# A second layer norm and router placed inside a rotary attention's tile pipeline

## The reference, cut to what matters

```
z = cond2(x)                       # dense and typed experts, mixed by a gate
z = z + attn(layernorm(z, ln1))    # convolution, rotary attention, 16 heads of 16, causal
z = z + moe(layernorm(z, ln2))     # 4 experts, each token goes to one of them
out = x + z

def _layernorm(x, w, b):
    mu = jnp.mean(x, axis=-1, keepdims=True)
    var = jnp.mean((x - mu) ** 2, axis=-1, keepdims=True)
    return (x - mu) * jax.lax.rsqrt(var + EPS) * w + b

def _moe(x, ln_w, ln_b, router_w, expert_wv, expert_proj):
    h = _layernorm(x, ln_w, ln_b)
    expert_idx = jnp.argmax(h @ router_w, axis=-1)
    ...
```

## Time and profile before

| what | value |
|---|---|
| median of 3 runs | 2254.34 us (2252.97 to 2255.35) |
| the profiled execution | 2255.13 us |
| its span, first to last instruction | 2253.3 us |
| mean granted TensorE clock | 0.956 |
| TensorE busy in the span | 2053.0 us, 91% |
| VectorE / ScalarE / GpSimd busy | 50% / 42% / 30% |
| rotary attention's tile loop | some 1876 to 1975 us |
| second norm and router | 1976 to 2017 us |
| sort and routed experts | 2017 us to the end |

### The profile page before, as it was taken

The page is one execution under the profiler, slowest core; times in us unless marked ns, Lnnn a source line. Parts: engine busy times, 40 slices in busy tenths (PEclk is TensorE's granted clock), DMA queues, the critical chain, the costliest instruction groups (busy, mean ns, idle before and its releaser), DMA issues. The chain is left out here.

```text
span 2253.3 us, 32388 instructions
## 1 busy us (share of the span) xinstructions
PE 2053.0 (91%) x11764; PEld 1725.6 (77%) x11764; DVE 1120.4 (50%) x1969; ACT 941.9 (42%) x1879; POOL 666.2 (30%) x713
## 2 busy tenths in 40 slices
PE   7999999999999999999998666899899666868998
PEld 6888888888888888888886455688799455747998
DVE  3333443434344344434435785423477566756775
ACT  4242323323232332424224697322355354555664
POOL 3030200203030120303100396110388143308884
PEclk9999999999999999999999698899899878978999
DMA  4010010101001010200001200410156123246661
GB/s 160 1 57 1 1 56 0 56 0 56 0 11 45 0 56 0 81 0 0 1 1 38 53 36 31 149 38 10 53 198 195 41 44 109 78 142 206 212 215 57
DMA packets 93436, 139.98 MB, mean 62 GB/s; under 512 B 15438, under 2 KB 70384, under 8 KB 93360
## 3 DMA queue, kind: packets, MB, share of 16 engines
q1 hardware_dynamic: 86304, 122.97, 17.1%
q0 software_dynamic: 4928, 12.86, 1.6%
q10 hardware_dynamic: 2128, 3.15, 0.4%
HBM read 106.96 MB, written 12.06 MB: 53 GB/s over the span
## 5 line engine op out<-in xcount | busy, mean ns | idle before, releaser
L584 DVE TENSOR_TENSOR cond_h<-cond_silu,ps 128x512 f32<-128x512 f32 x288 | 197.9, 687 | 697.6 <-ACT cond_silu L495 694.1
L495 ACT ACTIVATE cond_silu<-ps 128x512 f32<-128x512 f32 x288 | 172.3, 598 | 772.6 <-PE ps L414 772.6
L414 PE MATMUL ps<-a_x_hi,cond_w_hi 128*128 128x512 f32 x1152 | 449.8, 390 | 2.0 <-DVE a_x_lo L262 2.0
L414 PE MATMUL ps<-a_x_lo,cond_w_hi 128*128 128x512 f32 x1152 | 449.3, 390 | 0.0
L414 PE MATMUL ps<-a_x_hi,cond_w_lo 128*128 128x512 f32 x1152 | 449.1, 390 | 0.0
L383 POOL TENSOR_TENSOR cond_w_lo<-cond_stage_up,cond_w_hi 128x256 fp32r<-128x256 f32 x144 | 108.6, 771 | 833.7 <-ACT cond_w_hi L476 833.7
L414 PEld LDWEIGHTS ps<-a_x_hi,cond_w_hi 128*128 128x128 f32 x1152 | 216.9, 188 | 47.5 <-DVE a_x_lo L262 2.4
L414 PEld LDWEIGHTS ps<-a_x_hi,cond_w_lo 128*128 128x128 f32 x1152 | 216.9, 188 | 45.3
L414 PEld LDWEIGHTS ps<-a_x_lo,cond_w_hi 128*128 128x128 f32 x1152 | 216.9, 188 | 45.0
L430 PE MATMUL ps<-cond_h_hi,cond_d_hi 128*128 128x512 f32 x576 | 224.4, 390 | 3.4 <-DVE cond_h_lo L552 3.4
L430 PE MATMUL ps<-cond_h_hi,cond_d_lo 128*128 128x512 f32 x576 | 224.1, 389 | 0.0
(11 more groups left out here) (371 smaller groups left out, 4086.4 us busy)
## 6 DMA issues: line engine op xcount, KB each, us to landing
moe_stage_up<-in_L_ffn_expert_wv SPq DMA_DIRECT2D x22, 1024.0 KB, 8.4
typed_stage_up<-in_L_cond_wi SPq DMA_DIRECT2D x11, 1024.0 KB, 4.9
typed_stage_dn<-in_L_cond_wo SPq DMA_DIRECT2D x11, 1024.0 KB
moe_stage_dn<-in_L_ffn_expert_proj SPq DMA_DIRECT2D x11, 1024.0 KB
cond_stage_up<-in_L_cond_Wg SPq DMA_DIRECT2D x7, 1024.0 KB, 4.8
cond_stage_up<-in_L_cond_Wu SPq DMA_DIRECT2D x7, 1024.0 KB, 6.8
cond_stage_dn<-in_L_cond_Wd SPq DMA_DIRECT2D x7, 1024.0 KB, 5.1
hyp_v_now<-hyp_v_blk SPq DMA_DIRECT2D x16, 272.0 KB, 2.3
```

The source lines that it names most:

```text
L414: ins = pe.matmul(up_ps[st % 2][j], w[:, j, k, fs], x[:, k, tok], start=(i == 0), stop=(i == 3 * KC - 1))
L495: act.activation(silu[:, st % 2], up_ps[st % 2][0], ACT.Silu).then_inc(act_done, 1)
L584: dve.tensor_tensor(h[:, st % 2], silu[:, st % 2], up_ps[st % 2][1], ALU.mult).then_inc(up_free, 1)
```

## The change

The stage `layer_norm` is gone. Its work is done tile by tile in the rotary attention's pipeline, in token rows. `out` now takes the turned y as the stationary operand, so that its result has tokens on the partitions, and adds the residual by two matmuls with the identity. VectorE reads that result for bn_stats and bn_aggr (`stats`, `aggr`), ScalarE makes the inverse root by Ln and Exp (`rstd`), VectorE norms (`norm`) and adds x (`total`), GpSimd multiplies by w and adds b (`weigh`), TensorE turns h (`h_turn`), ScalarE copies it (`h_take`), TensorE makes the logits (`route`), VectorE keeps them (`keep`). SP copies the residual and x for each tile (`bring_sum`) and stores a tile's rows (`store`). The pipeline has 22 steps instead of 20, 8 of them ahead of the loop instead of 6. The choice is made once for all tokens behind the last tile; the first slot's weights are loaded at the start of `routed_ffn`.

```diff
+class Router:
+    def __init__(self, nc, ctx, ln_w, ln_b, w_r, x_rows, table, sel):
...
+        self.loads = [(self.w[:], wide(ln_w)), (self.b[:], wide(ln_b)), (self.wr[:], w_r.rearrange("(k p) e -> p k e", p=P))]
...
             lag = dict(bring=0, turn=1, q_blk=1, k_blk=1, score=1, clamp=2, top=2, shift=2, prob=2, p_turn=3, p_take=3,
-                       mix=3, y=3, y_turn=4, y_take=4, out=4, add=4, fetch=1)
-            order = dict(tensor="y_turn p_turn out turn mix score", scalar="y_take p_take q_blk prob",
-                         vector="clamp top add k_blk y", gpsimd="shift", sync="bring fetch")
+                       mix=3, y=3, y_turn=4, y_take=5, out=5, fetch=1, bring_sum=4, stats=5, aggr=5, rstd=5, norm=5, total=5,
+                       weigh=5, h_turn=6, h_take=6, route=6, keep=6, store=6)
+            order = dict(tensor="out p_turn h_turn turn mix score route y_turn",
+                         scalar="y_take p_take h_take q_blk rstd prob",
+                         vector="clamp top stats k_blk aggr norm total y keep", gpsimd="shift weigh",
+                         sync="bring fetch bring_sum store")
...
+            hT_ps, lg_ps = m.bank[0][:, D:2 * D], m.bank[1][:, D:D + E_MOE]
...
+                    def bring_sum(i, q, nth):
+                        wait(sp, out_done, i - 1)
+                        sp.dma_start(router.res[:, q], resT[:, :, bass.ds(i * P, P)]).then_inc(sum_brought[q], 16)
+                        wait(sp, added, i - 1)
+                        sp.dma_start(router.x[:, q], router.x_rows[bass.ds(i * P, P)]).then_inc(sum_brought[q], 16)
+                    def store(i, q, nth):
+                        sp.wait_ge(weighed, i + 1)
+                        sp.wait_ge(added, i + 1)
+                        sp.dma_start(router.table[bass.ds(i * P, P)], router.rows[:, q]).then_inc(stored[q], 16)
+                    if not hyper:
+                        router.load(sp)
+                    run(sp, "sync", dict(bring=bring, fetch=fetch, bring_sum=bring_sum, store=store))
...
                         wait(pe, k_blocked, i)
+                        if not hyper:
+                            wait(pe, kept, i - 5)
                         for c in range(KC):
...
                         wait(pe, q_taken, i)
+                        if not hyper:
+                            wait(pe, h_taken, i - 4)
                         for c in range(KC):
...
                         wait(pe, added, i)
+                        if not hyper:
+                            wait(pe, normed, i)
...
                     def out(i, q, nth):
                         pe.wait_ge(y_taken, i + 1)
                         wait(pe, added, i)
+                        if not hyper:
+                            wait(pe, normed, i)
+                            pe.wait_ge(sum_brought[q], 32 * (nth + 1))
+                            for k in range(KC):
+                                pe.matmul(o_ps, yT[:, q, k], wo[:, k], start=(k == 0), stop=False)
+                            for c in range(KC):
+                                ins = pe.matmul(o_ps[:, c * P:(c + 1) * P], router.res[:, q, c], m.ident, start=False, stop=(c == KC - 1))
+                            ins.then_inc(out_done, 1)
+                            return
                         for c in range(KC):
                             for k in range(KC):
                                 ins = pe.matmul(o_ps[:, c * P:(c + 1) * P], wo[:, k, c * P:(c + 1) * P], yT[:, q, k],
                                                 start=(k == 0), stop=(k == KC - 1))
                         ins.then_inc(out_done, 1)
 
+                    def h_turn(i, q, nth):
+                        pe.wait_ge(weighed, i + 1)
+                        wait(pe, h_taken, i)
+                        wait(pe, q_taken, i + 5 if not isinstance(i, int) else min(i + 5, NP))
+                        for c in range(KC):
+                            ins = pe.transpose(hT_ps[:, c * P:(c + 1) * P], router.rows[:, q, c * P:(c + 1) * P], m.ident)
+                        ins.then_inc(h_turned, 1)
+                    def route(i, q, nth):
+                        pe.wait_ge(h_taken, i + 1)
+                        wait(pe, kept, i)
+                        wait(pe, k_blocked, i + 6 if not isinstance(i, int) else min(i + 6, NP))
+                        for c in range(KC):
+                            ins = pe.matmul(lg_ps, router.hT[:, q, c], router.wr[:, c], start=(c == 0), stop=(c == KC - 1))
+                        ins.then_inc(routed, 1)
+                    if not hyper:
+                        pe.wait_ge(router.loaded, 16 * len(router.loads))
+                    run(pe, "tensor", dict(turn=turn, score=score, p_turn=p_turn, mix=mix, y_turn=y_turn, out=out, h_turn=h_turn, route=route))
...
+                    def inverse(i, q, nth):
+                        act.wait_ge(averaged, i + 1)
+                        wait(act, normed, i - 1)
+                        act.activation(router.rstd[:, q:q + 1], router.mean[:, q, 1:2], ACT.Ln, bias=router.eps[:]).then_inc(logged, 1)
+                        act.wait_ge(logged, i + 1)
+                        act.activation(router.rstd[:, q:q + 1], router.rstd[:, q:q + 1], ACT.Exp, scale=-0.5).then_inc(rstd_done, 1)
+                    def h_take(i, q, nth):
+                        act.wait_ge(h_turned, i + 1)
+                        wait(act, routed, i - 1)
+                        act.activation(router.hT[:, q].rearrange("p c n -> p (c n)"), hT_ps, ACT.Copy).then_inc(h_taken, 1)
+                    if not hyper:
+                        act.preload_act_table_set("natural_log_exp_and_others")
+                        act.wait_ge(eps_set, 1)
...
+                        if not hyper and not isinstance(i, int):
+                            dve.wait_ge(gathered, i + 1 + lag["k_blk"] - lag["stats"])
...
+                    def statistics(i, q, nth):
+                        dve.wait_ge(out_done, i + 1)
+                        wait(dve, rstd_done, i - 1)
+                        dve.bn_stats(router.stats[:, q], o_ps).then_inc(gathered, 1)
+                    def aggregate(i, q, nth):
+                        if isinstance(i, int):
+                            dve.wait_ge(gathered, i + 1)
+                        dve.bn_aggr(router.mean[:, q], router.stats[:, q]).then_inc(averaged, 1)
+                    def normalize(i, q, nth):
+                        dve.wait_ge(rstd_done, i + 1)
+                        wait(dve, weighed, i - 1)
+                        dve.tensor_scalar(router.xn[:, q], o_ps, router.mean[:, q, 0:1], router.rstd[:, q:q + 1],
+                                          ALU.subtract, ALU.mult).then_inc(normed, 1)
+                    def total(i, q, nth):
+                        dve.wait_ge(sum_brought[q], 32 * (nth + 1))
+                        wait(dve, stored[q], 16 * nth)
+                        dve.tensor_tensor(router.rows[:, q, D:], o_ps, router.x[:, q], ALU.add).then_inc(added, 1)
+                    def keep(i, q, nth):
+                        dve.wait_ge(routed, i + 1)
+                        dve.tensor_copy(router.logits[:, bass.ds(i, 1)].rearrange("p o e -> p (o e)"), lg_ps).then_inc(kept, 1)
+                    phases = dict(stretch=stretch, k_blk=block_k, clamp=clamp, top=top, y=scale_y, add=add)
+                    if not hyper:
+                        phases = dict(k_blk=block_k, clamp=clamp, top=top, y=scale_y, stats=statistics, aggr=aggregate, norm=normalize, total=total, keep=keep)
+                    run(dve, "vector", phases)
+                    if not hyper:
+                        dve.wait_ge(kept, NP)
+                        router.choose(dve, chosen)
...
+                    def weigh(i, q, nth):
+                        pool.wait_ge(normed, i + 1)
+                        wait(pool, stored[q], 16 * nth)
+                        wait(pool, h_turned, i - 1)
+                        pool.tensor_tensor(router.xn[:, q], router.xn[:, q], router.w[:], ALU.mult).then_inc(scaled, 1)
+                        pool.wait_ge(scaled, i + 1)
+                        pool.tensor_tensor(router.rows[:, q, 0:D], router.xn[:, q], router.b[:], ALU.add).then_inc(weighed, 1)
...
-def layer_norm(nc, m, tag, srcT, ln_w, ln_b, router, sync_late):
...
     def sync(self, sp):
+        self.slots.load_slot(sp, 0, 0)
...
-            attention(nc, m, "rope", False, s0, m.sumT, rope)
+            second.close()
+            router = Router(nc, s, a["L0_ffn_ln2_w"], a["L0_ffn_ln2_b"], a["L0_ffn_router_w"], typed_table, moe_table, m.moe_sel)
+            attention(nc, m, "rope", False, s0, m.sumT, rope, router, moe_stored)
...
-            with ExitStack() as f:
-                rows = f.enter_context(nc.sbuf_tensor("moe_rows", [P, NP, 2 * D], F32))
-                layer_norm(nc, m, "ln2", m.sumT, a["L0_ffn_ln2_w"], a["L0_ffn_ln2_b"],
```

(56 more changed lines are left out.)

189 lines of the change are left out of this document (18 added, 171 removed).

## The result

The changed kernel takes 2299.33 us (median of four, 2296.64 to 2301.72) against 2254.85 (four, 2252.97 to 2259.67): a ratio of 1.0194, 95% interval 1.0173 to 1.0215, so 44.5 us slower. The forecast was 2273.0 with a range up to 2288: the sign and the mechanism came, the size did not. The profiled execution took 2296.64 us, span 2294.8, 41.5 more than before; the clock's mean fell from 0.956 to 0.947.

The account below looks back on a forecast made before the run. Bound before: the ring of VectorE and the scores, 5.46 us a step. Loop 43.7 + drain 13.4 + loads 1.5 + choice 1.8 + barrier 0.9 - removed stage 42.4 = +18.9 us, giving 2273 us, range 2255 to 2288.

Parts of the forecast that it names:

- the sign: Whole kernel: the change makes it slower, +18.9 us; slower by more than 4.5 us given 0.80.
- the mechanism: Rotary attention loop: out waits about 2 us each time for copies queued on SP behind the fetch, which waits for mix.
- this ring: Loop's circle of out, p_turn, p_take, h_take, q transposes, mix, SP issues, landing: 9.1 us a step, +43.7 us over twelve.
- rival A: Loop: copies are in time, TensorE with ScalarE sets a step of 7.7 us; about 2255, no change; chance 0.12.
- The landing of x: Loop: the 128 KB copy lands 2.3 us after issue, bounds 2.1 to 3.5.
- rival C: Loop: TensorE's clock falls to 1.2 GHz, some 3.5 us more a step, +42, 2315 us; chance 0.06.
- the main case: Loop: clamps 9.1 us apart from the fifth on; 2273 us, own range 2264 to 2288; chance 0.74.
- Drain: From the last clamp through the last tile's keep: 25.7 us against 12.35 before, +13.4 us.
- the removed 42.4 us: Time from the last residual add to the sort's first matmul, which the change takes away: -42.4 us.
- choice and barrier: Behind the last tile: the choice standing alone, +1.8 us, and one barrier, +0.9 us.
- the first expert slot: Its loads, issued at the sort, are hidden by the sort: cost 0, upper end 3 us.
- the router's loads: Start of the pipeline: three loads issued ahead of the first x, 3 x 0.49 = +1.5 us.

Follow-up runs that it names:

- e1: Changed kernel with SP's order edited so bring_sum (the router's copies) is issued ahead of fetch: 2258.91 us.
- e4: Changed kernel with seven identity matmuls, result read by nobody, in front of out's wait for the copies: 2283.45 us.
- e5: e1 with p_turn ahead of out in TensorE's order: 2240.71 us, ratio 0.9928 to the kernel before.
- e8: e5 with unread identity matmuls where TensorE idles in the last steps behind the loop: 2239.39 us.
- e7: Changed kernel with p_turn ahead of out on TensorE, the copies still behind fetch on SP: 2264.47 us.
- e11: Changed kernel with two unread identity matmuls, instead of seven, ahead of out's wait for the copies: 2289.04 us.

## Why the prediction was wrong, by its own steps

- **The mechanism held.** `out` waits for router_x about 2.1 us each time, SP issues x 1.2 to 2.1 us behind the mix's end (1.4 forecast), VectorE is idle 22.4 of 46 us (a third forecast), the order on VectorE is covered. e1 showed that this ring is worth 40 us, and rival A's step of 7.7 came as 7.79 once it was taken away.
- **The ring's length**: 9.1 predicted, 9.32 in the three undisturbed steps: 12 x 0.2 = 2.6 us of the miss. The landing of x was 2.3 in the median, the value taken, with single ones up to 2.9. What was sized too short is the issue: x went out 1.6 us behind the mix's end in the median, and once, ahead of the 2.77 us wait above, the issue of `res` alone took 1.48 us.
- **The failed step is rival C's: "by the row of the first attention, which has such gaps too, the clock stays. Chance 0.06."** It didn't stay. 12 x (10.54 - 9.32) = 14.6 us of the loop are the clock (13.2 by the direct count over eleven steps), and e4, which fills the wait and leaves every order as it was, gives back 15.9, of which 12.6 in the loop. Two errors are in that sentence. The row of the first attention shows 12.90 us busy of 20 and a clock of 1.00, but not how its idle time lies: in that loop (1290 to 1370, the first lines below this list) the waits of a step are 1.3, 0.7 and 0.4 us in the mean, here they are 2.2 and 0.8. And the window from 1300 to 1320 leaves out that loop's first steps: from 1290 to 1300 the clock was 0.81, and there, in the last line below, the same eight p_turn matmuls took 1.88 us behind a wait of 1.83. Further, C was priced as another world (every step at 1.2 GHz, 2315) instead of as an addition to the main case. The clock fell in part of nine steps out of twelve, and even a step slow from `out` on lost 2.2 us and not the 3.5 of C, since the mix was at full clock again. A cost of 0 to 42 us on top of 2273 would have taken the range past 2300. The Trainium skill (TensorE: Matmul & The Clock Gate, "Why this matters for your kernels") warns that idle gaps between bursts bring the lower clock back. In direction the trace agrees (0.54 and 0.50 around a wait of 2.77 us), but the page words its warning for gaps longer than any wait in this loop, so the prediction's "by that rule it would be 2315" reads more into it than it says. Which pattern of waits brings the clock down is not settled by these runs.
- **Drain**: 25.7 predicted, 32.5 measured. The stretch up to the first `out` was 2.2 us against 1.7, and the four rounds were 7.5, 8.1, 6.1 and 8.7 us against 6.45, 6.45, 4.7 and 6.4, with `out` 1.8 to 2.1 us long in the last three and p_turn 1.92 in the first. The same rounds stand at full clock in other runs: the first took 6.25 us in e1 (from 1991.12 to 1997.37), the third 4.87 in e5 (1991.38 to 1996.25), the last 6.7 in e8. With these the drain would be 2.2 + 6.25 + 6.25 + 4.87 + 6.7 = 26.3 us, an estimate across runs: some 6 of the 6.8 us are the clock as well, so rival C's sentence is behind some 20 us of the miss and the sum of the phases was nearly right. That e4's drain is no shorter (32.7) doesn't speak against it: its seven matmuls stand ahead of each of the four `out`s there too, 1.7 to 2.7 us each time, 7.7 in all.
- **Right or nearly so**: the removed 42.4 us; choice and barrier 3.3 (2.7 predicted); the first expert slot costs nothing (235.7 us on both sides, though ScalarE's rounding starts 9.5 us behind the sort's start, the split starts 17.7 behind it against 17.5). **Wrong but small**: the router's loads cost +1.5 on paper and nothing in fact (first clamp 1880.79 against 1880.88).

The waits of TensorE in the first attention's loop, kernel before, and a row of its first steps:

```profile
PE ps L1106 <- ACT hyp_prob L1178: 13.4, 10, 1.8
PE ps L1119 <- ACT hyp_pT L1183: 6.5, 9, 0.9
PE ps L1139 <- ACT hyp_yT L1188: 3.7, 9, 0.5
```

```profile
1293.65 1.88 PE L1106 MATMUL ps<-const,hyp_prob 128*128 128x128 f32 x8 [1.83 <-ACT hyp_prob L1178]
```

Sum of the misses: 14.6 (clock in the loop) + 2.6 (ring) + 6.8 (drain) + 0.6 (choice and barrier) - 1.6 (loads) - 0.4 (the first three distances) = 22.6 us, which is the 41.5 of the span less the 18.9 forecast. The medians stand 44.5 us apart; those 3 us more are between executions.

## What to carry to other kernels

Before a transfer is put behind another on a queue, ask what the one ahead waits for: here a copy that nothing held back stood behind a fetch that waited for the mix, and moving one word gave back 40 of the 44.5 us. When a predicted wait stops TensorE in every step, price the wait and a lower clock together, for the work behind it, and look for a row of the kernel before that shows the clock behind a wait of the same length. When a phase is moved ahead of a wait, follow the circle once more: in e7 it was shorter and not gone. When a wait is gone, read the list of waits again: the next entry (y_take ahead of `out`) was worth another 18 us and made the fused kernel faster than the one before.

## What the runs showed of the hardware

TensorE's idle time cost more than its length: matmuls whose result nobody reads, put into a wait that stayed, made the program 15.9 us faster, and the granted clock in the loop went from 0.81 to 1.00. A mean busy share didn't tell which clock is granted: e1 had 1.00 at 36.00 busy us of 46, e11 0.96 at 33.99, and the changed kernel 0.81 at 34.36, of which a part is busy only because it ran slowly. Nor did the wait just ahead: in e11 a wait of 0.96 us had a slow `out` behind it and one of 1.07 us a fast one.
